# Four graph layers on one core: block steps of layers 2 and 3 moved in among the dense products

## The reference

```python
def _L2_gnn_ref(x, edge_src, edge_dst, edge_weight, eps, w1, b1, w2, b2):
    msgs = edge_weight[:, None] * x[edge_src]
    agg = jax.ops.segment_sum(msgs, edge_dst, num_segments=N)
    h = (1.0 + eps[0]) * x + agg
    h = jax.nn.relu(h @ w1 + b1)
    return h @ w2 + b2

# layer 3, with self loops added to src and dst
    norm = dinv[src] * dinv[dst]
    h = x @ W.T
    out = jax.ops.segment_sum(norm[:, None] * h[src], dst, num_segments=n) + b
    h = relu(layer_norm(out, gamma, beta))

x = _layernorm(x + _L2_gnn_ref(...)); x = _layernorm(x + _L3_gnn_ref(...))
```

## Time and profile before

| | us |
|---|---|
| median of 3 runs (lowest, highest) | 3699.97 (3696.57, 3700.96) |
| the profiled execution | 3701.64 |
| its span | 3700.3 |
| PE, DVE, ACT, POOL busy | 2884.8, 1939.4, 1266.9, 2466.3 |
| granted TensorE clock over the span | 0.885 |

### The profile page before, as it was taken

One profiled execution on the slowest core, in us unless ns is written; L12 is line 12 of the kernel. 1 busy time (PEld: TensorE's weight loads), 2 busy tenths in 40 slices (PEclk: granted clock), 3 DMA queues, 4 the chain that ended last, 5 costly groups with the idle time before them and its releaser, 6 DMA issues.

```text
span 3700.3 us, 59110 instructions
## 1 busy us (share of the span) xinstructions
PE 2884.8 (78%) x18909; PEld 2107.1 (57%) x18926; DVE 1939.4 (52%) x6744; ACT 1266.9 (34%) x3547; POOL 2466.3 (67%) x2275
## 2 busy tenths in 40 slices
PE   3989887778888548799957985689886674799974
PEld 2777665557666437444436773367665563555553
DVE  6888776767777438422243334422354445122278
ACT  3566676667877526300050002500021113000035
POOL 2877877777776735577737775677777771777772
PEclk9999998889999868899958996589998886899987
DMA  7677677778888748687726774755554445777764
GB/s 270 85 149 133 101 151 144 146 160 171 188 175 185 132 142 267 183 242 235 221 81 175 226 224 118 228 172 184 164 146 134 137 144 194 243 229 222 220 193 143
DMA packets 499789, 652.69 MB, mean 176 GB/s; under 512 B 80686, under 2 KB 441564, under 8 KB 494748
## 3 DMA queue, kind: packets, MB, share of 16 engines
q0 software_dynamic: 153600, 258.41, 34.3%
q1 hardware_dynamic: 307130, 367.02, 31.0%
q10 hardware_dynamic: 38754, 23.48, 2.1%
HBM read 434.19 MB, written 214.52 MB: 175 GB/s over the span
## 4 chain that ended last, share of the span: by engine, by line
POOL 29%; PE 27%; issue 16%; DVE 11%; DMA 8%; ACT 7%; DVEq 1%; SPq 1%; ACTq 0%; POOLq 0%
POOL rows_buf L791 25%; PE PSA L823 8%; PE PSA L879 4%; PE PSA L1222 3%; DMA A<-rows_buf,big 3%; PE PSA L1338 2%; DVE accT L1382 2%; POOL A L1518 2%; ACT accT L1404 1%; PE PSA L1206 1%; PE PSA L1329 1%; DMA A<-accT 1%; ACT S L1182 1%; POOL rows_buf L1923 1%; DVE big L1301 1%
## 5 line engine op out<-in xcount | busy, mean ns | idle before, releaser
L1518 POOL DMA_INDIRECT A<-rows_buf,big x572 | 901.2, 1576 | 374.0 <-issue 156.3
L791 POOL DMA_INDIRECT rows_buf<-T,idx x888 | 850.0, 957 | 311.4 <-issue 270.4
L879 PE MATMUL PSA<-S,rows_buf 128*128 128x128 bf16 (+2 forms) x5904 | 604.5, 261 | 247.2 <-DMA rows_buf<-X,idx 125.9
L879 PEld LDWEIGHTS PSA<-S,rows_buf 128*128 128x128 bf16 (+2 forms) x5904 | 546.2, 148 | 334.7 <-DMA rows_buf<-X,idx 105.9
L941 DVE TENSOR_TENSOR accT<-PSA,accT 128x256 f32 (+2 forms) x354 | 132.6, 375 | 1013.1 <-PE PSA L879 999.8
L791 POOL DMA_INDIRECT rows_buf<-X,idx x528 | 506.6, 959 | 174.0 <-issue 158.7
L1382 DVE TENSOR_TENSOR accT<-PSA,accT 128x392 f32 (+5 forms) x366 | 239.9, 656 | 181.9 <-issue 56.4
L1222 PE MATMUL PSA<-XRS,rows_buf 128*128 128x256 f32 x1144 | 312.0, 397 | 6.8 <-ACT rows_buf L1232 6.8
L742 ACT ACTIVATE accT<-accT,vec 128x500 f32<-128x500 f32 (+3 forms) x26 | 17.7, 694 | 696.6 <-DVE accT L740 696.6
L1232 ACT ACTIVATE rows_buf<-PSA 128x512 f32<-128x512 f32 x286 | 167.9, 594 | 204.0 <-PE PSA L1222 172.0
L1222 PEld LDWEIGHTS PSA<-XRS,rows_buf 128*128 128x128 f32 x1144 | 209.1, 197 | 33.0 <-issue 9.3
(11 more groups left out here) (305 smaller groups left out, 5785.2 us busy)
## 6 DMA issues: line engine op xcount, KB each, us to landing
XRS<-Ad SPq DMA_DIRECT2D x144, 512.0 KB
Ad<-accT SPq DMA_DIRECT2D x28, 1568.0 KB, 7.1
rows_buf<-Ad SPq DMA_DIRECT2D x72, 512.0 KB
XRS<-in_xpad SPq DMA_DIRECT2D x192, 128.0 KB
XRS<-X SPq DMA_DIRECT2D x192, 128.0 KB, 3.1
A<-accT SPq DMA_DIRECT2D x3, 6272.0 KB
Awd<-accT SPq DMA_DIRECT2D x6, 3136.0 KB, 10.2
rows_buf<-T,idx POOLq DMA_INDIRECT x888
```

Of the source, the lines that this page charges most:

```text
L791: s_hg[i % RING][j // 2].on(pool.indirect_dma_start(Gv(i % RING, j), None, table, bass.IndirectOffsetOnAxis(idx[:, c:c + 1], 0)), 16)
L879: last = pe.matmul(PS[i % 2][0:F, W * h:W * h + W], Gv(i % RING, j)[:, o:o + F], hits[:, i % SRING, j, :], start=j + part == 0, stop=j == ...
L1518: pool.indirect_dma_start(A, bass.IndirectOffsetOnAxis(tgt[:, c:c + 1], 0), G[:, i % RING, j, :], None, compute_op=ALU.add).then_inc(s_k[n ...
```

## The change: what it does

- In layer 2 and layer 3 the tail's steps are emitted from the first group on, up to two per group, beside the dense pieces.
- Blocks enter the pipeline in the order in which they become complete, by the last cold group and the last quad that can reach their nodes (`last_group`, `last_quad`), two groups after that. A step in which no block enters still moves the others on (`tail_steps`).
- `PACE2` goes from 54 to 100, `PACE3` from 70 to 84.
- Stages are fused: layer 2's tail is now 13 steps deep, layer 3's 11. Layer 2's first stage takes one block.
- To stand beside the table, the tail's buffers move out of the part of `big` that holds it; in layer 3 they lie in the weights that are no longer needed, now one tensor. Their rings shrink from 24 slots to 12 (`ZL`) and 8 (`ZT`). Layer 2 keeps one pair of PSUM banks for the quads instead of two.
- The residual's loads and the tail's stores go from SP's queue to ACT's.
- The first row of a dense window is held within bounds that follow from how dst is drawn (`window_range`), so that the program may know which blocks a quad can reach.

The code, cut to its core:

```diff
-PACE2 = 54
-PACE3 = 70
+PACE2 = 100
+PACE3 = 84
...
-ZL = 24
+ZL = 12
+ZT = 8
...
+def window_range(w):
+
+    at = N * (BND[w] * 128 / E) ** 2
+    return max(0, math.floor(at) - 125), min(LAST, math.ceil(at) + 125)
...
-    late = big[:, 0:ZL * D].rearrange("p (r d) -> p r d", d=D)
-    hid = big[:, ZL * D:ZL * D + 2048].rearrange("p (r o n) -> p r o n", r=2, o=2)
-    TBL = big[:, ZL * D + 2048:ZL * D + 2048 + 1536].bitcast(BF16).rearrange("p (r n) -> p r n", r=4)
+    beyond_x = big[:, 2 * LAST:2 * LAST + AW]
+    late = beyond_x[:, 0:ZL * D].rearrange("p (r d) -> p r d", d=D)
+    hid = beyond_x[:, ZL * D:ZL * D + 512].rearrange("p (r o n) -> p r o n", r=2, o=2)
...
+    last_z = weights[:, 1024:1024 + ZT * D].rearrange("p (r d) -> p r d", d=D)
...
+    for w in range(NWIN):
+        lo, hi = BND[w], BND[w + 1]
+        least, most = window_range(w)
+        done = v.tensor_scalar(wb[:, lo:hi], cm[:, lo:lo + 1].broadcast_to([128, hi - lo]), float(least), float(most), ALU.max, ALU.min)
+    link(done)
     s_d.by(sc)
     for w in range(NWIN):
-        lo, hi = BND[w], BND[w + 1]
-        first = sc.activation(bwi[0:1, w:w + 1], cm[0:1, lo:lo + 1], ACT.Identity)
...
+    s_tb = s_zero + [s_w]
...
+    block = list(range(NT))
+    brows = lambda t: rows(block[t])
+    bcols = lambda t: cols(block[t])
+
+    def tail_steps(stages, ring, written, stored):
+
+        stages = sorted(stages, key=lambda x: -x[0])
+        entered = []
+        now = [0]
+
+        def step(ready):
+
+            n, k = now[0], len(entered)
+            if k < NT and ready(block[k]) and (k < ring or n + written >= entered[k - ring] + stored + 2):
+                entered.append(n)
+            at = {n - e: k for k, e in enumerate(entered)}
+            for lag, f in stages:
+                if lag in at:
+                    f(at[lag])
+            now[0] += 1
+            return len(entered) < NT or n < entered[-1] + stages[0][0]
+
+        return step
...
+    def residual(src, queue=sp):
...
+            s_ld[t % 4].mark(t, queue.dma_start(XR[0:brows(t), t % 4, :], src[bcols(t), :]), 16)
...
+    def normalise_tail(lag, ring, w, given, done):
+
+        bn, ag, root, rec, neg, norm = (f for _, f in normalise(0, ring, w, given, done))
+
+        def statistics(t):
+            bn(t)
+            ag(t)
+
+        def scales(t):
+            rec(t)
+            neg(t)
+
+        return [(lag, statistics), (lag + 1, root), (lag + 2, scales), (lag + 3, norm)]
...
-            if b == 0 and q >= 2:
+            if b == 0 and q >= pairs:
                 if by_rows is None:
-                    s_hqa.by(pe, Q0 + per * (q - 1))
+                    s_hqa.by(pe, Q0 + per * (q - pairs + 1))
                 else:
...
+        def last_group(t):
+
+            return max((i for i in range(n) if lowest(cold[i]) < 128 * t + rows(t)), default=-1)
+
+        def last_quad(t):
+
+            return max((w // per for w in range(nw) if window_range(w)[0] < 128 * t + rows(t) and window_range(w)[1] + W > 128 * t),
+                       default=-1)
+
         def ready(t):
 
-            return next((i for i in range(n - 1) if lowest(cold[i + 1]) >= 128 * (t + 1)), n - 1)
+            return max(last_group(t), after[last_quad(t)] if last_quad(t) >= 0 else -1)
 
         def added(engine, t):
 
-            s_hqa.by(engine)
-            s_hacc.by(engine, C0 + ready(t) + 1)
+            if last_quad(block[t]) >= 0:
+                s_hqa.by(engine, Q0 + per * (last_quad(block[t]) + 1))
+            if last_group(block[t]) >= 0:
+                s_hacc.by(engine, C0 + last_group(block[t]) + 1)
 
         if steps is not None:
             remains()
             rounds()
+            block[:] = sorted(range(NT), key=lambda t: (ready(t), t))
+            for c in Count.every:
+                c.at.clear()
+            tail = steps(added)
         streams()
-        todo = steps(added) if steps is not None else []
-        quads = max(after.values())
         for i in range(n):
             gather(i)
             products(i)
             sums(i)
             if beside is not None and 0 <= i - LEAD < NT:
                 beside(i - LEAD)
-            if steps is not None and i == quads + 1:
-                s_hdn.by(sp)
-            if steps is not None and i > quads + 1:
-                for x in range(2):
-                    if todo and ready(todo[0][0]) + 2 <= i:
-                        todo.pop(0)[1]()
-        for _, step in todo:
-            step()
+            for x in range(2 if steps is not None else 0):
+                tail(lambda t: ready(t) + 2 <= i)
+        if steps is not None:
+            while tail(lambda t: True):
+                pass
+            block[:] = range(NT)
...
-        added(pe, min(t + 3, NT - 1))
-        lo, n = 128 * t, min(512, N - 128 * t)
+        added(pe, t)
+        if t >= 1:
+            s_uc.of(pe, t - 1)
         for o in range(2):
-            i = t // 2 + o
-            if i >= 2:
-                s_uc.of(pe, i - 2)
             for h in range(2):
-                ins = pe.matmul(PS[6 + i % 2][:, 0:n], M1[:, h, 128 * o:128 * o + 128], accT[:, h, lo:lo + n], start=h == 0, stop=h == 1)
-            s_u.mark(i, ins)
+                ins = pe.matmul(PS[6 + o][:, 0:brows(t)], M1[:, h, 128 * o:128 * o + 128], accT[:, h, bcols(t)], start=h == 0, stop=h == 1)
+        s_u.mark(t, ins)
...
-        return pipeline_steps(
-            [(0, lambda t: hidden(t, added)), (1, hidden_out), (1, residual(X2)), (3, bias_residual),
-             (4, multiply(lambda t: [(hid[:, t // 4 % 2, h, 128 * (t % 4):128 * (t % 4) + rows(t)], M2[:, h, :]) for h in range(2)],
-                          lambda t: s_uc.of(pe, 2 * (t // 4) + 1))),
-             (5, add_biased)]
-            + normalise(6, ZL, 0, s_z, s_nm)
-            + [(12, store(ZL, X3)), (12, by_degree), (13, high), (13, transpose(lambda t: XS[0:rows(t), t % 4, :], s_xs)),
-               (14, turned(accT))] + parts(14, T3, D, turned_and_high, TBL, v, X=XS, n=4), lambda t: t // 4 * 4 + 3)
-
+        return tail_steps(
+            [(0, lambda t: hidden(t, added)), (0, residual(X2, sc)), (1, hidden_out),
+             (2, multiply(lambda t: [(hid[:, t % 2, h, 0:brows(t)], M2[:, h, :]) for h in range(2)],
+                          lambda t: s_uc.of(pe, t), banks=(4,))), (2, bias_residual), (3, add_biased)]
+            + normalise_tail(4, ZL, 0, s_z, s_nm)
+            + [(8, store(ZL, X3, sc)), (8, by_degree), (9, high), (9, transpose(lambda t: XS[0:brows(t), t % 4, :], s_xs, (5,))),
+               (10, turned(accT, banks=(5,)))] + parts(10, T3, D, turned_and_high, TBL, v, queue=sc, X=XS, n=4), ZL, 3, 8)
+
+    s_z.by(sc)
     hybrid(X2, D, wide, HWIN, 2, lambda part, h, b: X2s[:, b, 128 * h:128 * h + 128], lambda: load_table(X2, X2s),
-           lambda slot, j: G2[:, slot, j, :], [rb[:, 4096:5632], rb[:, 5632:7168], rest], Awd, per=3, split=1, weighted=True,
-           paced=PACE2, steps=second_tail)
+           lambda slot, j: G2[:, slot, j, :], [rb[:, 4096:5632], rb[:, 5632:7168], weights[:, 0:1536]], Awd, per=3, split=1,
+           weighted=True, paced=PACE2, steps=second_tail, pairs=1)
...
-        return pipeline_steps([(0, lambda t: multiply3(t, added)), (1, convolved)] + normalise(2, ZL, 1, s_a1, s_n1)
-                              + [(9, gamma), (10, beta), (8, residual(X3)), (11, relu_residual3)]
-                              + normalise(12, ZL, 0, s_z, s_nm) + [(18, store(ZL, out))])
+        return tail_steps([(0, lambda t: multiply3(t, added)), (1, convolved)] + normalise_tail(2, ZT, 1, s_a1, s_n1)
+                          + [(4, residual(X3, sc)), (6, scaled)] + normalise_tail(7, ZT, 0, s_z, s_nm) + [(11, store(ZT, out, sc))],
+                          ZT, 1, 11)
 
     T3s = big[:, 0:NT * 384].bitcast(BF16).rearrange("p (b n) -> p b n", n=768)
     hybrid(T3, D, wide, 16, 1, lambda part, h, b: T3s[:, b, D * part + 128 * h:D * part + 128 * h + 128],
-           lambda: load_table(T3, T3s), ring(0, D), buffers(6144), Ad, paced=PACE3, steps=third_tail)
+           lambda: load_table(T3, T3s), ring(0, D),
+           [rb[:, 6144:7168].bitcast(BF16), XS.rearrange("p r d -> p (r d)").bitcast(BF16), weights[:, 0:1024].bitcast(BF16)],
+           Ad, paced=PACE3, steps=third_tail)
```

More of the change, by code:

```diff
@@ L200 @@
 class Count:
+    every = []
     def __init__(self, nc, name):
+        self.every.append(self)
         self.sem = nc.alloc_semaphore(name)
@@ L578, in pipeline, with multiply @@
                 between[n]()
+    block = list(range(NT))
[16 more added lines that the diff above has]
+        return step
     def zs(ring, t):
-        return (late if ring == ZL else rows_buf)[0:rows(t), t % ring, :]
-    def residual(src):
+        return {ZL: late, ZT: last_z}.get(ring, rows_buf)[0:brows(t), t % ring, :]
+    def residual(src, queue=sp):
         def load(t):
             if t >= 4:
-                s_z.of(sp, t - 4)
```

(19 more changed lines are left out.)

110 lines of the change are left out of this document (53 added, 57 removed).

## The result

The changed kernel takes 3636.21 us, median of 4 runs (3635.54 to 3644.43), against 3700.22 us (4 runs); the ratio is 0.9836, interval 0.9822 to 0.9849. In a second measurement it took 3645.48 us (3641.31 to 3645.73, 3 runs; ratio 0.9843, 0.9823 to 0.9863). Forecast was 3655 us, range 3625 to 3692. The profiled execution is the slowest of the first four: 3644.43 us, span 3643.2. What follows is read from that one, so its stages add up to 57 us less than before, not to the 64 us of the medians.

The account below looks back on a forecast made before the run. It took POOL's pace to bound layer 2's groups, PE layer 3's full stretch, then DVE. 3700.3 us less 16 (layer 2's last steps), plus 4 (its groups), less 33 (layer 3) gave 3655 us, range 3625 to 3692.

Parts of the forecast that it names:

- Rivals 1, 3 and 4: Layer 3 gives half back, 3688 us (0.20); layer 2 turns to PE, 3725 (0.05); early steps come late, about 3685 (0.04).
- Rival 2: Everything hides: POOL alone sets layer 3, last gather at 3603, steps of 1.3 us, total 3627 us; chance 0.11.
- my sum: The forecast's added terms: layer 3's last gather at 3622, whole span 3655 us.
- the signs that I named: Layer 2's gathers 660 to 686 us, T3 store 30 to 34, layer 3's stretch 410, its end 33; wrong: DVE 90%.
- The steps behind layer 2's last group: After layer 2's last group, 22 steps in 42.5 us become 16 at 1.65 us, saving 16 us (bounds 11 and 22).
- the turn to layer 3: From layer 2's last store to layer 3's first gather: 24 us, expected to stay.
- Layer 2's groups: Layer 2's gathers stay at POOL's pace, with a loss of 4 us (bounds 6 won, 20 lost).
- Layer 3's full stretch: Layer 3 up to group 84: PE just stays the bound, 398 us of work and 12 of waits, 410 us.
- Behind it: After layer 3's last piece: 48 us for nine groups, 22 for the last 14 steps, 4 to the span's end.
- At nothing: First-row limits, fused stages, smaller rings and layer 2's single pair of PSUM banks: booked as costing nothing.

Follow-up runs that it names:

- f2: Changed kernel with four empty stages more in layer 2's tail, 20 steps behind the last group instead of 16: 3639.42 us, ratio 0.9837.
- g3: Changed kernel with layer 2 on the old schedule (no block before the last quad, natural order, PACE2 54), one-block steps kept: 3664.75 us, ratio 0.9902.
- g4: Changed kernel with only PACE3 back to 70, blocks still early: 3666.12 us, ratio 0.99.
- f1: Changed kernel with layer 3 on the old schedule (no block before the last quad, natural order, PACE3 70), short pipeline kept: 3728.73 us, ratio 1.0077.
- g2: f1 with layer 3's fused stages taken apart by phase within a step: 3688.74 us, ratio 0.9967.
- g1: Changed kernel with layer 3's fused stages taken apart by phase within a step, depth, rings, order and pace kept: 3627.19 us, ratio 0.9802.
- e1: Changed kernel with layer 3 on the old schedule and PACE3 70, new pipeline kept, on the slower-gather chip: 4060.82 us, ratio 1.012.

## Why the prediction was right, and where its sizes were off

The mechanism held: most blocks fit beside the pieces, PE stayed full there, and POOL's pace in layer 2 hardly suffered. The time was 19 us below the forecast by the median, and 12 us by the profiled execution, whose span is what the sum forecasts. Rivals 1, 3 and 4 did not come about. Rival 2 did in half: layer 3's gathers went at POOL's pace (477.5 us, 5.08 per group), and the last one came at 3606.4, where the rival had 3603 and my sum 3622. Its short end, 24 us behind that gather, did not come: it took 36.8. Its 3627 us are 9 below the median, which is nearer than my 3655.

Of the signs that I named, two came out otherwise: T3's last store landed 23.7 us after the last group's addition, not 30 to 34, and DVE was at 91% from the last gather to its last operation (77% to the end of the span), where I had called 90% a sign of being wrong.

**The steps behind layer 2's last group: mis-sized.** I saved 16 us, as 22 steps less 16 of 1.65 us. It is 22.7 us from gather to gather. A step costs 1.12 us on the mean (17.9 us from the addition to the last store's issue, by 16), but f2 shows that this is no price: four steps more leave the time where it was. The term should have been the chain of work behind the last group. That the turn to layer 3 stays was right.

**Layer 2's groups: about right.** Booked at +4 us, measured +6.1. Which kernel it is to be held against I had not seen: with the new pipeline on the old schedule the same gathers take 693 us (g3), so the early start and `PACE2` together are worth some 20 us here, which the comparison with the kernel before hides. The clock did not spoil it. The rule of the Trainium skill (TensorE: Matmul & The Clock Gate, the part on the HAM clock gate) that only busy work holds the full rate agrees with the trace in direction, 0.94 to 0.89 in the first window where PE became less busy, and 0.86 to 0.91 in the second where it became more. Spread evenly, it gave back in one what it took in the other.

**Layer 3's full stretch: 9 us too dear.** 410 us forecast from the first piece to the products of group 84; measured 400.7 (3169.1 to 3569.8), with PE at 98% and 0.99. The sum of PE's work, 398 us, was about right (394.3 busy in the trace). The 12 us of waits were mis-sized: PE was idle 6.4 us in all, 4.4 of them for DVE, and DVE waited 183.7 us for PE, so it was seldom late. The pace, which I had not priced by itself, is worth 20 to 30 us (g4).

**Behind it: right in the sum, in part by luck.** 48 + 22 + 4 = 74 us forecast, measured 50.2 (3569.8 to the last addition at 3620.0) + 18.8 (to the last normalise) + 4.4 = 73.4. The 48 were POOL's 45 and 3 for the last addition, with DVE's 40 hidden under them. In the trace it is the other way round: POOL is through at 3606.4, and the last addition comes 13.6 us later, since PE waits 15.5 us for one-hots that DVE writes late. The first such wait, the 4.65 us before 3575.41, is behind the last quad's additions on DVE and a pause of 2.5 us in which its sequencer reads the addresses of the next 14 groups (L972). In the trace 14 blocks' products follow the short piece, one of them right behind group 84; the 13 named ahead of the prediction leave that one out.

**"At nothing": wrong for the fused stages.** They cost DVE time in every block: in f1 the 49 blocks take 51.5 us more, of which g2 gives 35 back, 0.7 us a block. I had booked neither this nor that the new pipeline on the old schedule would be 43 us slower in layer 3. In the changed kernel most blocks stand beside pieces where DVE waits anyway (183.7 us in the stretch), so mainly the last 14 show it: g1 takes 9 us off the end, and 9 to 18 us off the whole by the medians on other chips. I had looked at how many DVE operations a block has, and not at what stands next to what. The row limits were not tested by themselves; up to layer 2's first gather the trace is 1.4 us longer than before. The smaller rings may be part of the 17 us that g2 leaves open. For the single pair of PSUM banks no wait of PE for a quad's eviction is among the long ones of layer 2.

What stays open: which part of the new pipeline shortens layer 2's end; what its own fused stages, which g1 leaves as they are, cost; what `PACE2` does alone; why executions differ by some 10 us in the earlier stages; how much of the gain the changed kernel keeps on the chip where gathers are slower. Moving the residual's loads back to SP's queue beside the pieces was not tried; I expect nothing of it, since they would stand behind pieces that wait for the very blocks they serve.

## What to carry to other kernels

Work that follows a stage bound by another engine belongs beside it, spread at an even rate; catch-up at two per group made two engines wait for each other in each round (g3). Price what is left behind the last group by its chain of work, not by steps times a price, and check a long piece of the chain against the waits before shortening it. When stages of a software pipeline are merged, keep operations of different items next to each other on the engine: taking the merged stages apart by phase won 9 us or more at the same depth, and 40 where all blocks follow the pieces.

## What of the hardware was not expected

- On DVE (traces of the kernel before and of f1), an operation that reads the result of the one just before it starts later: 0.42 to 0.46 us behind it instead of 0.33 for 128x256 in f32, and 0.19 instead of 0.07 for 128x1.
- On one chip the kernel before took 4010 us, on the others 3700. The instructions' durations on POOL were the same (946 ns); a group's gathers took 6.1 us instead of 5.1 in layer 2, at 203 GB/s instead of 240 in a stretch of equal code. Its traces put part of POOL's waits before a gather (238.1 us in e1) down to releases from outside the core ("remote"), which name no cause.
